# Contexts turned two blocks at a time, four 64-row copies behind them, and new order tables

## The reference, cut to what matters

```python
h = concatenate([tok(x), txt], axis=1)                 # 16 x 165 x 256
h = h + attn(layernorm(h))
h = h + ffn(layernorm(h))
# attn: 16 query heads, 4 key/value heads, 16 features per head, RoPE
scores = einsum('bqhd,bkhd->bhqk', xq, keys) / sqrt(16)
scores = where(|q - k| <= 32, scores, -inf)
ctx = einsum('bhqk,bkhd->bqhd', softmax(scores), values).reshape(b, s, 256)
return ctx @ Wo
# ffn: bit_linear(256 -> 1024), depthwise conv of 3 taps, silu, bit_linear(1024 -> 256);
# bit_linear: activations rounded to 8 bits by their row maximum, weights to -1, 0, 1
```

## Time and profile before

| | |
|---|---|
| median of three runs | 397.09 us |
| the profiled execution, whole | 396.99 us |
| its span, first to last instruction | 395.2 us |
| PE / PEld / DVE / ACT / POOL busy | 92 / 69 / 76 / 65 / 54 % of the span |
| mean granted PE clock | 0.987 of full speed |

### The profile page before, as it was taken

The page is one execution under the profiler, slowest core; times in us unless marked ns, Lnnn a source line. Parts: engine busy times, 40 slices in busy tenths (PEclk is TensorE's granted clock), DMA queues, the critical chain, the costliest instruction groups (busy, mean ns, idle before and its releaser), DMA issues.

```text
span 395.2 us, 8402 instructions
## 1 busy us (share of the span) xinstructions
PE 364.5 (92%) x3033; PEld 273.6 (69%) x3037; DVE 301.8 (76%) x639; ACT 256.5 (65%) x483; POOL 215.0 (54%) x245
## 2 busy tenths in 40 slices
PE   6799799999999999999989999999999988987886
PEld 2376557777877886678767876788678866853743
DVE  2246649654599879888998698959895998799795
ACT  3213436568786779677868686769767966672552
POOL 5406589688479928892689427971994006001000
PEclk9889989999999999999999999999999999999999
DMA  7671521201000012002000220022011100000101
GB/s 235 166 181 41 153 99 29 54 13 28 20 19 2 2 48 50 22 21 53 19 0 2 57 48 2 2 61 44 11 27 44 27 2 13 25 2 0 35 2 35
DMA packets 21907, 16.71 MB, mean 42 GB/s; under 512 B 12435, under 2 KB 20936, under 8 KB 21865
## 3 DMA queue, kind: packets, MB, share of 16 engines
q1 hardware_dynamic: 20970, 15.11, 15.3%
q10 hardware_dynamic: 895, 1.06, 1.0%
HBM read 9.82 MB, written 3.38 MB: 33 GB/s over the span
## 4 chain that ended last, share of the span: by engine, by line
PE 65%; DVE 17%; ACT 7%; issue 5%; DMA 4%; POOL 1%; SPq 1%; DVEq 0%; ACTq 0%; POOLq 0%
PE bank L1784 8%; PE bank L1864 8%; PE bank L1835 7%; PE bank L1878 6%; PE bank L1937 5%; PE bank L1938 4%; PE bank L1907 4%; DMA shared<-in_x 4%; PE bank L1855 3%; PE bank L1731 3%; PE bank L1981 3%; DVE shared L1635 2%; PE bank L1898 2%; PE bank L1797 2%; PE bank L1847 2%
## 5 line engine op out<-in xcount | busy, mean ns | idle before, releaser
L1501 DVE TENSOR_REDUCE mx<-bank 120x4 fp32r<-120x376 f32 (+3 forms) x88 | 44.1, 506 | 26.8 <-PE bank L1847 26.2
L1273 ACT COPY pT<-bank 94x480 f32<-94x480 f32 (+3 forms) x88 | 48.1, 554 | 21.7 <-PE bank L1864 21.3
L1265 ACT ACTIVATE pr<-bank 120x376 f32<-120x376 f32 (+3 forms) x88 | 39.6, 453 | 27.1 <-PE bank L1855 26.2
L1864 PE MATMUL bank<-cst,pr 120*94 120x120 f32 (+3 forms) x352 | 51.3, 270 | 2.6 <-ACT pr L1265 2.5
L1835 PE MATMUL bank<-kbd,q_hl 128*120 128x376 f32 (+3 forms) x176 | 51.1, 374 | 1.6 <-issue 0.9
L1113 POOL TENSOR_TENSOR rs<-ve,half_neg 110x3 f32<-110x3 f32 x16 | 16.7, 1044 | 62.8 <-DVE ve L1529 47.2
L1937 PE MATMUL bank<-xT_hi,w1T 128*128 128x330 f32 x128 | 44.2, 351 | 1.3 <-DVE late L1584 0.9
L1864 PEld LDWEIGHTS bank<-cst,pr 120*94 120x94 f32 (+3 forms) x352 | 36.1, 122 | 10.0 <-ACT pr L1265 6.0
L1120 POOL TENSOR_SCALAR xn<-h,mv,rs 110x256 f32<-110x256 f32 x21 | 27.6, 1321 | 25.3 <-PE bank L1772 24.9
L1135 POOL TENSOR_TENSOR rc<-qk,cst 110x320 f32<-110x320 f32 x22 | 20.0, 908 | 38.9 <-ACT qk L1236 37.9
L1938 PE MATMUL bank<-xT_lo,w1T 128*128 128x330 f32 x128 | 39.5, 314 | 0.0
(11 more groups left out here) (131 smaller groups left out, 877.7 us busy)
## 6 DMA issues: line engine op xcount, KB each, us to landing
kbd<-shared SPq DMA_DIRECT2D x56, 41.2 KB, 2.1
out<-h SPq DMA_DIRECT2D x7, 330.0 KB
wn<-in_w SPq DMA_DIRECT2D x2, 1024.0 KB, 6.6
shared<-in_x SPq DMA_DIRECT2D x4, 432.0 KB
h<-in_txt SPq DMA_DIRECT2D x1, 770.0 KB
late<-in_lin SPq DMA_DIRECT2D x1, 768.0 KB, 7.6
vw<-v_rows SPq DMA_DIRECT2D x8, 94.0 KB
v_rows<-qk SPq DMA_DIRECT2D x8, 82.5 KB
```

The lines of the kernel that those rows point to most:

```text
L1265: nc.scalar.activation(pr[:, g % 3, 0:HKV * WIDTH[j]], S_BANKS[g % 2][0:QP, 0:HKV * WIDTH[j]], ACT.Exp, scale=HD ** -0.5).then_inc(exped, 1)
L1273: nc.scalar.copy(pT[0:WIDTH[j], g % 3, :], S_BANKS[g % 2][0:WIDTH[j], 0:HKV * QP]).then_inc(p_kept, 1)
L1501: nc.vector.tensor_reduce(mx[:, g % 4, :].bitcast(F32R), S_BANKS[g % 2][0:QP, 0:HKV * WIDTH[j]].rearrange("p (k c) -> p k c", k=HKV), axis ...
L1864: o = nc.tensor.transpose(S_BANKS[g % 2][0:w, kv * QP:(kv + 1) * QP], pr[:, g % 3, kv * w:(kv + 1) * w], ident[0:QP, 0:QP])
```

## The change: what it does

1. `select` is one plain transpose for two blocks. Two blocks' 64 features each stand side by side as 128 columns, and one transpose of 120 rows by 128 columns brings them to 128 rows (block, key head, feature) by 120 columns (token, query head). A group of 4 has two such transposes, the group of 3 has one of 128 and one of 64 columns. Before, there were two products of 120 by 64 by 60 for each block: 22 products for a pair against 6 transposes now.
2. The rows now say which block and the columns which head, so `keep_sel` is four copies of 64 rows: for each block parity and each head parity, from rows of one half to rows of the same or the other half. The semaphore is raised by the last of the four.
3. All rows of `ORDER` and several of `ONCE` have new ticks, on PE, DVE, ACT, POOL and SP.

```diff
@@ keep_sel, ACT @@
-                nc.scalar.copy(ctxP[:, :, js[0] * QB:(js[-1] + 1) * QB],
-                               N_BANK[:, 0:len(js) * QP // 2].rearrange("p (q c) -> p c q", c=2)).then_inc(sel_kept, 1)
+                at = js[0] * QB
+                turned = N_BANK[:, 0:(len(js) + 1) // 2 * QP].rearrange("p (i q c e) -> p e c i q", q=QB, c=2, e=2)
+                for odd in range(2):
+                    cnt = (len(js) + 1 - odd) // 2
+                    for e in range(2):
+                        dst = ctxP[QK * e:QK * (e + 1), :, at:at + len(js) * QB].rearrange("p c (j q) -> p c j q", q=QB)
+                        o = nc.scalar.copy(dst[:, :, odd::2, :], turned[QK * odd:QK * (odd + 1), e, :, 0:cnt, :])
+                o.then_inc(sel_kept, 1)
@@ select, PE @@
-                half = QP // 2
-                for c in range(len(GROUPS[k])):
-                    for e in range(2):
-                        o = nc.tensor.matmul(N_BANK[QK * e:QK * (e + 1), c * half:(c + 1) * half], ctxn[:, c, :],
-                                             ident[0:QP, e:QP:2], start=True, stop=True)
+                cnt = len(GROUPS[k])
+                for c in range(0, cnt, 2):
+                    src = ctxn[:, c:min(c + 2, cnt), :].rearrange("p c v -> p (c v)")
+                    o = nc.tensor.transpose(N_BANK[0:QK * min(2, cnt - c), c // 2 * QP:(c // 2 + 1) * QP], src,
+                                            ident[0:QP, 0:QP])
                 o.then_inc(ctx_picked, 1)
@@ ORDER, 'pe.context', first row of eight @@
-        (32, 33, 38, 40, 48, 57, 63, 64, 75, 84, 85),
+        (36, 37, 38, 42, 56, 57, 64, 65, 73, 85, 86),
```

More of the change, by code:

```diff
@@ L143 @@
     'pe.turn_xn': (
-        (5, 6),
-        (18, 20),
+        (4, 5),
+        (19, 21),
         (69, 72),
[L147 to L151, removed]
+        (137, 141),
+        (211, 218),
+        (286, 295),
+        (371, 376),
+        (448, 451),
     ),
@@ L154 @@
         (8, 9, 10),
[L155 to L161, removed]
+        (24, 27, 29),
+        (76, 82, 89),
+        (147, 156, 167),
+        (225, 238, 247),
+        (301, 308, 318),
+        (378, 391, 401),
+        (458, 462, 475),
     ),
@@ L164 @@
         (13, 14, 17),
[L165 to L171, removed]
+        (33, 46, 60),
+        (102, 114, 126),
+        (191, 198, 202),
+        (255, 257, 277),
+        (325, 342, 358),
+        (414, 420, 434),
+        (486, 496, 509),
     ),
@@ L255 @@
         (205,),
-        (280,),
-        (359,),
+        (283,),
+        (361,),
         (436,),
-        (514,),
-        (584,),
+        (516,),
+        (583,),
         (613,),
@@ L284 @@
         (182,),
-        (259,),
-        (338,),
-        (412,),
-        (492,),
-        (564,),
+        (260,),
+        (337,),
+        (413,),
+        (491,),
+        (563,),
         (611,),
@@ L293 @@
     'pe.down': (
-        (194, 195, 197),
-        (270, 271, 272),
-        (348, 349, 354),
-        (425, 427, 428),
-        (502, 503, 505),
-        (573, 574, 575),
+        (193, 196, 201),
+        (271, 272, 276),
+        (350, 351, 355),
+        (425, 426, 427),
+        (504, 505, 506),
+        (573, 576, 578),
         (612, 614, 615),
-        (626, 627, 628),
+        (626, 626, 626),
     ),
     'dve.stats1': (
-        (5,),
+        (4,),
         (9,),
         (13,),
-        (17,),
-        (37,),
-        (101,),
-        (149,),
-        (198,),
+        (21,),
+        (53,),
+        (100,),
+        (150,),
+        (199,),
     ),
     'dve.norm1': (
-        (6,),
+        (5,),
         (),
@@ L383 @@
     'dve.max_x': (
-        (50,),
-        (94,),
-        (143,),
-        (192,),
+        (48,),
+        (93,),
+        (142,),
+        (193,),
         (242,),
-        (289,),
-        (338,),
+        (290,),
+        (337,),
         (377,),
@@ L424 @@
         (68, 79),
-        (119, 128),
-        (167, 178),
-        (217, 226),
-        (263, 274),
-        (312, 322),
+        (118, 129),
+        (166, 177),
+        (215, 226),
+        (263, 275),
+        (314, 322),
         (362, 369),
@@ L433 @@
     'dve.fold_g': (
-        (78, 83),
-        (126, 132),
-        (172, 181),
-        (224, 230),
-        (272, 279),
+        (75, 83),
+        (127, 133),
+        (176, 181),
+        (224, 231),
+        (271, 279),
         (323, 327),
@@ L443 @@
     'dve.max_g': (
-        (81, 84),
-        (130, 133),
-        (174, 182),
-        (229, 232),
-        (275, 280),
-        (325, 329),
-        (371, 374),
+        (82, 85),
+        (132, 134),
+        (180, 183),
+        (230, 232),
+        (274, 280),
+        (325, 328),
+        (370, 374),
         (404, 406),
@@ L520 @@
-        (271, 280, 283),
-        (326, 334, 338),
+        (9, 11, 12),
+        (24, 27, 29),
+        (54, 60, 67),
+        (105, 113, 126),
+        (161, 170, 177),
+        (214, 219, 227),
+        (268, 277, 286),
+        (323, 334, 340),
     ),
     'act.keep_q': (
-        (14, 15, 17),
-        (37, 39, 44),
-        (75, 85, 87),
-        (127, 137, 139),
-        (181, 192, 194),
-        (237, 245, 249),
-        (290, 298, 303),
-        (344, 354, 357),
+        (15, 17, 19),
@@ L532 @@
+        (32, 40, 45),
+        (76, 84, 87),
+        (135, 139, 141),
+        (181, 182, 193),
+        (233, 246, 250),
+        (291, 301, 304),
+        (343, 354, 357),
     ),
     'act.keep_k': (
-        (16, None),
-        (46, 49),
-        (89, 93),
-        (144, 148),
-        (198, 201),
-        (250, 257),
+        (18, None),
+        (47, 49),
+        (89, 92),
+        (143, 146),
+        (195, 198),
+        (251, 255),
         (307, 311),
-        (358, 362),
+        (359, 360),
@@ L587 @@
-        (243,),
-        (297,),
+        (81,),
+        (134,),
+        (190,),
+        (245,),
+        (298,),
         (351,),
-        (401,),
+        (400,),
         (),
@@ L593 @@
     'act.high_x': (
-        (92,),
-        (143,),
-        (196,),
-        (251,),
+        (91,),
+        (144,),
+        (199,),
+        (252,),
         (305,),
-        (360,),
+        (361,),
         (406,),
@@ L633 @@
     'act.conv_g': (
[L634 to L635 removed]
+        (132, 133),
+        (188, 189),
         (241, 242),
@@ L703 @@
     'sp.load_v': (
-        (3,),
-        (6,),
+        (5,),
+        (7,),
         (9,),
-        (13,),
+        (11,),
         (14,),
-        (18,),
-        (21,),
+        (16,),
+        (20,),
         (23,),
@@ L717 @@
         (12,),
-        (16,),
-        (19,),
+        (15,),
+        (18,),
         (22,),
-        (25,),
+        (24,),
     ),
     'sp.store': (
-        (11,),
-        (15,),
+        (13,),
         (17,),
-        (20,),
-        (24,),
+        (19,),
+        (21,),
+        (25,),
         (26,),
```

231 lines of the change are left out of this document (110 added, 121 removed), and 168 rows, old and new, of the table ORDER.

## The result

The changed kernel took 386.99 us, median of four runs (386.33 to 388.36), against 397.06 us of the kernel before beside it: ratio 0.974 [0.968, 0.980], 10 us less. Run again later, five times, it was at 0.969 [0.966, 0.972], 385.86 against 397.91 us. The forecast was 390, with 384 to 393 as the range of its likeliest case. So the time lies where it was expected. Of the terms that led there, PE's 17.7 us roughly hold, but the share of them that reaches the time does not, and neither does the price of the copies.

What follows compares the result with a forecast made beforehand. PE bounds the middle stretch: of its 17.7 us saved, 11 on the chain, less 0.6 for ACT and a third for waits, leave 7 us off 396.99. Forecast 390 us, range 382 to 401, likeliest case 384 to 393.

Steps and rivals of the forecast that it cites:

- PE's 17.7 us: PE, whole program: the most that the shorter select and contexts moved together give back; at least 8.9 us.
- What bounds the kernel: Middle stretch, 60 to 340 us: PE in flight for 270.1 of 280 us, so PE savings count there, little elsewhere.
- the 17 that the prediction set as its mark: PE's time in flight in the middle was to fall by less than 17 us, since waits fill some.
- The price of a narrow step: PE at context products: 0.27 us for each trip there and back; 75 places become 49, 7.0 us less.
- PE holds 65% of the chain, so 11 us are on it: Middle stretch: of some 17 us saved on PE, 11 us shorten the path, by PE's chain share.
- a third off for waits: Middle stretch: DVE and ACT become the next to wait for, so a third comes off, leaving 7 us.
- The contexts' part: PE's context products moved together, 75 places to 49: 7.0 us less PE time, bounds 0 and 7.0.
- `select`'s 10.7 us: PE at `select`: 8.9 us less from two transposes a group, 1.8 us less in front of the step.
- the contexts' gain is given back: Rival, 28%: contexts stand later, groups finish later, only select's 8.9 us count; 394 us.
- The four copies: ACT at `keep_sel`: 0.71 us a group of four, 8.0 us more in all, upper bound 19.5; 0.6 given back.
- ACT decides: Rival, 15%: at `keep_sel` in the middle, copies add 19.5 us, half before something PE awaits; 403 us.
- The clock: Rival, 2%: a fifth of the middle stretch runs at PE's half clock, 20 us lost; 410 us.

Runs made afterwards that it cites:

- the tail: Measuring tail behind the changed kernel's last step, PE groups of wide transposes, context products and both selects: a narrow trip costs 0.14 + 0.16 us.
- new tables: The change with the old `select` and the old single copy: 389.74 against 399.55 us of the kernel before, ratio 0.977.
- contexts apart: The change with 23 context steps moved by one place each, 49 places to 72: 392.2 against 385.86 us of the change beside it.
- a single copy: The change with one copy of 128 rows for the four of 64 rows, output in wrong order: 383.4 us, ratio 0.961 to the kernel before.
- the last tail: Tail behind the change, eight blocks of score products, shift and turned probabilities singly, in pairs, in fours: 7.45, 7.45 and 7.44 us.

## Why the prediction was right, and where it was not

**What bounds the kernel** was right: PE in the middle stretch. All the gain lies there (296.5 to 283.8 us). PE is in flight for 12.3 us less (364.5 to 352.2), under the 17 that the prediction set as its mark.

**The price of a narrow step** was right: 0.27 us against 0.30 in the tail and 0.23 to 0.28 in the whole kernel. So was `select`'s: 0.20 us for two transposes, and 0.55 less than before with what is saved in front of it.

**"PE holds 65% of the chain, so 11 us are on it", and a third off for waits** was the step that was mis-sized. It turned 17.7 us into 7. The contexts' part reaches the time nearly in full: 23 places are worth 5.3 to 6.3 us. `select`'s 10.7 us reach it with 6.3, which is near 65%, so there it is the further third that was wrong. The chain's share of an engine says what that engine held in one path; nothing ties it to the fraction of a saving that arrives, and the two parts had different ones. What did tell was the idle time: the span is PE's time in flight and its idle time, and idle stayed at 30.7, 30.0, 32.0 and 31.9 us in before, new tables, change, and contexts apart. But time in flight holds short waits too, those that end before the last record has. With the new tables, from the start of the step before each `select` to the start of the step behind it, 24 `select`s hold PE for 30.5 us with the old form and for 21.4 with the new one and a single copy. So 9.1 us arrive on the spot, and 6.3 at the end: of the three that are lost further on, idle time shows one (30.0 to 31.0), and two lie in time in flight.

**The rival "the contexts' gain is given back"** (28%) was wrong for this change and right for its edit alone. With the order of before around them, contexts moved together give nothing, since PE waits for maxima and exponentials instead. What the new order seems to add is other work in that place: two blocks' scores, maxima and turned probabilities stand side by side, so one block's steps can cover the other's way over DVE and ACT. That pairing gains PE nothing by itself, as the last tail shows. But with it PE is idle for 32 us whether the contexts stand together or apart, and without it for 30.7 us when they stand apart and 38.8 when together. That it is the pairs which do this, and nothing else in the new tables, was not tried alone.

**The four copies** were mis-sized twice. A group takes 1.05 us, not 0.71: the overlap that I took from the earlier trace rows exists only between copies that stay in the same half of the rows, on both sides. There a group takes 0.72, the prediction's own figure. Over the program ACT was busy for 15.5 us more in the copies (23.7 against 8.2), near the upper bound of 19.5. The Trainium skill (ScalarE: Activation LUTs, What ACT_TABLE_LOAD costs) has ACTIVATEs overlap by about 93 ns back to back; the runs agree where the half stays (0.25 us long, 0.15 to 0.16 apart) and not where it changes (0.27 apart). The price for the time was about 3 us (3.3, give or take 2), not 0.6: a fifth of their busy time, not 7%. The row of waits shows a part of it: PE sat 2.2 us before `out_proj`, where it had sat 0.6 in the kernel before. About half of the difference stands before the very last `out_proj`, where only filler lies between it and its `select` (1.22 us for 0.43):

```profile
  PE bank L1907: 0.6, 2
```

**The rival "ACT decides"** (15%) had its condition met, a group above 1.0 us, and gave no slower kernel. It took half of the copies' time as on the path; about a fifth was. In the order of before, though, with fewer steps between `select` and `out_proj`, the same copies make the kernel 1.2% slower. The rival was right for that kernel.

**The clock** did fall once in the middle of the first profiled execution, for part of ten us, and that stretch took some 1.7 us longer. The new transposes don't bring this by themselves, since the same program run again kept full clock over the same steps. The Trainium skill (TensorE: Matmul & The Clock Gate, Part 4: PE-mode transpose) says that transposes don't count as busy for the clock in the same way; no run here shows a stretch that lost the clock to them.

**The sum as it was measured**: tables 9.4 us less, of which 26 places are 6 to 7 (an estimate from the 23 that were set apart); `select` with its copies free 6.3 less; copies 3.3 more: 12.4 us. These are steps from one ratio to the next, so they add up to the change's 0.969 by construction, and the sum is no check of them. Medians give 12.0 (397.91 to 385.86), and the first comparison 10. The prediction had about 7 us for the 17.7 of PE, where 15.7 were measured for tables and `select` together, and 0.6 for the copies, where 3.3 were. Its factors were too low for PE and for ACT alike, and the two errors in part made up for each other: that the forecast was only 3 us too high by the first comparison, and 5 by the second, is in part luck. What stays open is the tables' remaining 2 to 3 us, and where on its way the rest of `select`'s saving is spent.

## What to carry to other kernels

When one engine is in flight for nine tenths of a stretch, count what an edit takes out of its start-to-start distances and ask next whether its waits stay the same, those that show as idle time and the short ones that don't. To answer it, look at what stood between a step and the answer it waits for; here a saving that removed cover was worth nothing until the order put other work there. A total over several instructions divided by their number is a distance only where nothing waits among them. And let two edits be timed apart: here one was slower alone and faster behind the other.

## What the runs showed of the hardware

- A PE step of products that write 32 rows each costs 0.14 us when PE goes to it (0.55 for 0.41 before it) and 0.16 when it comes back (0.37 for 0.21); going to one that writes 64 rows also costs 0.14. Between steps that write 94 rows or more a change of kind, type or size costs nothing that can be seen (7.45 and 7.44 us for 24 and 6 changes).
- ACT copies of 120 elements a row from one bank start 0.15 to 0.16 us apart in the same half of the rows (0.72 us for four), and 0.27 us apart as soon as source or target half differs from that of the copy before (1.05 us for four). To copy from one half to the other costs nothing in itself, and 128 rows take hardly longer than 64 (2.31 against 2.23 us for twelve).
- The same kernel showed full clock in one execution and a mean of 0.66 for ten us in another, behind waits of the same length.
